# A decay mix with a routed low-rank layer: half of the base product of the first two groups computed early, stored, and added to by DMA

## What is computed

```
a[t] = a[t-1]*decay + exp(f[t])*f[t]      (forward and backward, the same for b with exp(f[t]))
y    = sigmoid(x) * (a_fwd + a_bwd + ...) / (b_fwd + b_bwd + ...) * gain
h      = silu(y @ rw1.T + rb1)                       64 hidden channels
logits = h @ rw2.T + rb2 + gates                     16 experts, top 2, softmax -> coeff
xa     = y @ A.T                                     256 = 16 experts x rank 16
out    = x + y @ W.T + bias + (xa * coeff) @ B.T
```

## Time and profile before

| | |
|---|---|
| median of 3 runs | 720.68 us (720.63 to 720.79) |
| profiled execution, its own time | 720.62 us |
| its span in the trace | 718.8 us |
| busy: PE, DVE, POOL, ACT | 597.5 (83%), 528.0 (73%), 352.2 (49%), 349.3 (49%) us |
| matmuls | 2626 |

### The profile page before, as it was taken

One profiled execution on the slowest core, in us unless ns is written; L12 is line 12 of the kernel. 1 busy time (PEld: TensorE's weight loads), 2 busy tenths in 40 slices (PEclk: granted clock), 3 DMA queues, 4 the chain that ended last, 5 costly groups with the idle time before them and its releaser, 6 DMA issues.

```text
span 718.8 us, 6928 instructions
## 1 busy us (share of the span) xinstructions
PE 597.5 (83%) x2626; PEld 486.8 (68%) x2626; DVE 528.0 (73%) x547; ACT 349.3 (49%) x401; POOL 352.2 (49%) x164
## 2 busy tenths in 40 slices
PE   0005342498999999999999999999999999999998
PEld 0003231386888688868886888778887888888886
DVE  7999999799788979796979796979698713021302
ACT  4777876845574556435664565356735420002000
POOL 1789988744754575356536553655464511000100
PEclk9999665599999999999999999999999999999999
DMA  5324442313350435041613261226214310231031
GB/s 181 117 86 143 141 142 88 118 59 117 127 167 30 146 103 191 29 147 59 224 41 120 86 208 56 74 104 209 83 50 138 95 55 1 88 110 38 0 89 73
DMA packets 30865, 74.22 MB, mean 103 GB/s; under 512 B 4464, under 2 KB 4592, under 8 KB 30832
## 3 DMA queue, kind: packets, MB, share of 16 engines
q1 hardware_dynamic: 30832, 73.79, 30.8%
HBM read 57.00 MB, written 16.78 MB: 103 GB/s over the span
## 4 chain that ended last, share of the span: by engine, by line
PE 59%; DVE 16%; POOL 16%; issue 6%; ACT 2%; DMA 0%; DVEq 0%; SPq 0%; POOLq 0%; ACTq 0%
PE acc L707 18%; PE acc L708 18%; PE acc L709 18%; POOL mix L461 5%; DVE mix L534 4%; DVE yr L560 3%; POOL kv L451 3%; POOL yr L456 3%; POOL y_lo L465 2%; POOL wx_lo L471 2%; DVE mix L539 2%; DVE xo L567 2%; PE acc L719 2%; PE acc L718 2%; ACT y_hi L314 1%
## 5 line engine op out<-in xcount | busy, mean ns | idle before, releaser
L707 PE MATMUL acc<-y_hi,wa_hi 128*128 128x512 f32 x640 | 257.3, 402 | 10.5 <-DVE xo L567 10.5
L708 PE MATMUL acc<-y_lo,wa_hi 128*128 128x512 f32 x640 | 253.5, 396 | 0.0
L709 PE MATMUL acc<-y_hi,wa_lo 128*128 128x512 f32 x640 | 253.2, 396 | 0.0
L707 PEld LDWEIGHTS acc<-y_hi,wa_hi 128*128 128x128 f32 x640 | 123.0, 192 | 43.6 <-DVE xo L567 18.2
L709 PEld LDWEIGHTS acc<-y_hi,wa_lo 128*128 128x128 f32 x640 | 122.7, 192 | 26.4
L708 PEld LDWEIGHTS acc<-y_lo,wa_hi 128*128 128x128 f32 x640 | 123.0, 192 | 24.9
L461 POOL TENSOR_TENSOR mix<-mix,kv 128x1024 f32<-128x1024 f32 x31 | 74.1, 2390 | 90.6 <-DVE mix L518 73.7
L718 PE MATMUL acc<-y_hi,wr 128*128 128x512 f32 x64 | 27.3, 426 | 99.3 <-POOL wa_lo L439 63.6
L567 DVE SCALAR_TENSOR_TENSOR xo<-acc,bias_sb,xo 128x512 f32<-128x512 f32 x64 | 46.7, 736 | 76.5 <-PE acc L709 76.4
L465 POOL TENSOR_TENSOR y_lo<-yr,y_hi 128x1024 fp32r<-128x1024 f32 x32 | 76.6, 2395 | 49.9 <-ACT y_hi L314 49.9
L471 POOL TENSOR_TENSOR wx_lo<-xa,wx_hi 128x512 fp32r<-128x512 f32 x16 | 20.4, 1298 | 152.6 <-ACT wx_hi L373 152.6
(11 more groups left out here) (85 smaller groups left out, 767.4 us busy)
## 6 DMA issues: line engine op xcount, KB each, us to landing
kv<-f_cm SPq DMA_DIRECT2D x32, 512.0 KB, 3.3
yr<-x_cm SPq DMA_DIRECT2D x32, 512.0 KB, 3.3
xo<-x_cm SPq DMA_DIRECT2D x64, 256.0 KB, 4.0
out<-xo SPq DMA_DIRECT2D x64, 256.0 KB, 3.5
xo<-w_base SPq DMA_DIRECT2D x5, 512.0 KB, 3.5
xa<-w_base SPq DMA_DIRECT2D x3, 512.0 KB, 4.3
xa<-w_router_a SPq DMA_DIRECT2D x2, 480.0 KB, 3.4
xo<-w_expert SPq DMA_DIRECT2D x1, 512.0 KB, 3.8
```

The source lines that it names most:

```text
L707: nc.tensor.matmul(out_ap, wh, yh, start=start, stop=False)
L708: nc.tensor.matmul(out_ap, wh, yl, start=False, stop=False)
L709: return nc.tensor.matmul(out_ap, wl, yh, start=False, stop=stop)
```

## The change

- TensorE first computes the base product of groups 0 and 1 (16 output blocks, "parts" p) over kc = 0 to 3 only: parts 0 to 4 as the units arrive, parts 5 to 15 one after the other, each when a bank has been drained (`part_out`).
- ScalarE copies each part from PSUM to `xo[2 + p % 4]` (`drain_part`) in steps 4 to 7; the copies stand after `exp_k` or at the end of the step (`part_steps`). SyncE stores each to `out` (`store_part`).
- Groups 0 and 1 then compute the base product only over kc = 4 to 7 (`base_from`). Their evacuated blocks are no longer stored by SyncE but added to `out` by an accumulating DMA that GpSimd issues (`add_out`), 3 at the end of step q = 2 and 5 at the end of the step in which the group ends, behind `p1(s+1)`.
- Groups 0 and 1 have 3 steps each: G0 in steps 8 to 10, its blocks 3 to 7 in step 11; G1 in 11 to 13, its blocks 3 to 7 in step 14; step 15 has no group; from G2 (step 16) on all is as before. Late splits start with unit 17.
- All even groups run `hid`, both `low_rank` and base block 0 with kc outermost, base block 0 three kc behind; its last three kc come after `spread`. Base block 2 comes before `spread` in even groups.

```diff
-banks = [(0, 1, 2, 3, 4)]
+banks = [(1, 2, 3, 4, 0)]
+
+SPLIT = 2
+HALF = CB // 2
+PARTS = SPLIT * CB
+PBUF = 4
+part_steps = {4: (0, 0, 2), 5: (2, 5, 7), 6: (7, 10, 12), 7: (12, 15, 16)}
+
+def base_from(G):
+    return HALF if G < SPLIT else 0
+
+def first_step(G):
+    return (CB, CB + 3)[G] if G < SPLIT else CB + 4 * G
+
+def last_step(G):
+    return first_step(G) + (3 if G < SPLIT else 4)
+
+tasks_at = {first_step(G) + q: (G, q) for G in range(GROUPS) for q in range(3)}
+ends_at = {last_step(G): G for G in range(GROUPS)}
+
+def quarter(s):
+    return tasks_at.get(s, (-1, -1))
+
+def held(g):
+    return g >= 2 * CB and g % CB in (1, 5)
+
+def stores_to(slot, end):
+    return sum(1 for e in range(PARTS, end) if e % XBUF == slot)
...
-def quarter(g):
-    return divmod(g - CB, 4) if g >= CB else (-1, -1)
...

     def load_x(e):
         if e >= XBUF:
-            sp.wait_ge(out_stored[e % XBUF], 16 * (e // XBUF))
+            if e - XBUF < PARTS:
+                sp.wait_ge(out_added[e % XBUF], 16 * (e // XBUF))
+            else:
+                sp.wait_ge(out_stored[e % XBUF], 16 * stores_to(e % XBUF, e))
         sp.dma_start(xo[:, e % XBUF, :], at(x_cm, e)).then_inc(x_in[e % XBUF], 16)

     def store(e):
         if e + AHEAD < GROUPS * CB:
             load_x(e + AHEAD)
-        sp.wait_ge(evacuated, e + 1)
-        sp.dma_start(at(out, e), xo[:, e % XBUF, :]).then_inc(out_stored[e % XBUF], 16)
+        if e >= PARTS:
+            sp.wait_ge(evacuated, e + 1)
+            sp.dma_start(at(out, e), xo[:, e % XBUF, :]).then_inc(out_stored[e % XBUF], 16)
+
+    def store_part(p):
+        sp.wait_ge(part_out, p + 1)
+        sp.dma_start(at(out, p), xo[:, 2 + p % PBUF, :]).then_inc(part_stored[p % PBUF], 16)
         sp.dma_start(dst, src).then_inc(late_in, 16)
     for s in range(STEPS):
-        if q == 2 and G < GROUPS:
+        ended = ends_at.get(s, -1)
+        early = 5 if ended < SPLIT else 6
+        if ended >= 0:
+            for j in range(3, early):
+                store(ended * CB + j)
+        if q == 2:
             store(G * CB)
         if 1 <= s < UNITS - 1:
             load_k(s + 1)
+        if s - 1 in part_steps:
+            for p in range(part_steps[s - 1][1], part_steps[s - 1][2]):
+                store_part(p)
         for n in chunks_at(load_steps, s):
             load_chunk(n)
-        if q == 0 and G > 0:
-            for j in range(6, CB):
-                store((G - 1) * CB + j)
-        if q == 2 and G < GROUPS:
-            for j in range(1, 3):
-                store(G * CB + j)
+        if ended >= SPLIT:
+            for j in range(early, CB):
+                store(ended * CB + j)
+        if q == 2:
+            store(G * CB + 1)
+            if G >= SPLIT:
+                store(G * CB + 2)
         if 1 <= s < UNITS - 1:
             load_r(s + 1)
+        if s in part_steps:
+            for p in range(part_steps[s][0], part_steps[s][1]):
+                store_part(p)
         for n in chunks_at(load_late_steps, s):
             load_chunk(n)
+        if 0 <= ended < SPLIT:
+            for j in range(early, CB):
+                store(ended * CB + j)
+        if q == 2 and G < SPLIT:
+            store(G * CB + 2)
         if s == CB:
             sp.wait_ge(w_lo_ready, CHUNKS - 1)
+            for i in range(PBUF):
+                sp.wait_ge(part_stored[i], 16 * (PARTS // PBUF))
             for e in range(AHEAD):
                 load_x(e)
     for i in range(XBUF):
-        sp.wait_ge(out_stored[i], 16 * len(range(i, GROUPS * CB, XBUF)))
+        sp.wait_ge(out_added[i], 16 * len(range(i, PARTS, XBUF)))
+        sp.wait_ge(out_stored[i], 16 * stores_to(i, GROUPS * CB))
...
+    def drain_part(p):
+        act.wait_ge(part_done, p + 1)
+        if p >= PBUF:
+            act.wait_ge(part_stored[p % PBUF], 16 * (p // PBUF))
+        nc.scalar.copy(xo[:, 2 + p % PBUF, :], acc[:, p % 5, :]).then_inc(part_out, 1)
+
...
-        late_split = s > 0 and (s - 1) % CB in (1, 5) and s > CB
+        routed = G >= 0
+        late_split = held(s - 1)
...
+        if s in part_steps:
+            for p in range(part_steps[s][0], part_steps[s][1]):
+                drain_part(p)
         if s < UNITS and q != 1:
             sigmoid_r(s)
             exps()
+        if s in part_steps:
+            for p in range(part_steps[s][1], part_steps[s][2]):
+                drain_part(p)
         if 0 < s <= UNITS and late_split:
             split_hi(s - 1)

...
+    def add_out(e):
+        pool.wait_ge(evacuated, e + 1)
+        pool.wait_ge(part_stored[e % PBUF], 16 * (e // PBUF + 1))
+        nc.gpsimd.dma_start(at(out, e), xo[:, e % XBUF, :], accum_op=ALU.add).then_inc(out_added[e % XBUF], 16)
+
...
             p1(s + 1)
+        ended = ends_at.get(s, -1)
+        if 0 <= ended < SPLIT:
+            for j in range(3, CB):
+                add_out(ended * CB + j)
+        if q == 2 and G < SPLIT:
+            for j in range(3):
+                add_out(G * CB + j)
         if s == CB - 2:
...
-        routed = 0 <= G < GROUPS
-        ending = q == 0 and G > 0
+        routed = G >= 0
+        ended = ends_at.get(s, -1)
+        ending = ended >= 0
         if ending:
-            evacuate(G - 1, 3)
-            evacuate(G - 1, 4)
+            evacuate(ended, 3)
+            evacuate(ended, 4)
...
+        if a == 1 and kc < base_from(G):
+            last.then_inc(slot_free, 1)
...
-        return three(acc[:, out_bank(G, j), :], wa_hi[:, kc, c], wa_lo[:, kc, c], yh, yl, kc == 0, False)
+        return three(acc[:, out_bank(G, j), :], wa_hi[:, kc, c], wa_lo[:, kc, c], yh, yl,
+                     kc == base_from(G), False)
+
+    def base_part(p, kc):
+        G, j = divmod(p, CB)
+        yh, yl = y_of(G, kc)
+        c = slice(ER + j * P, ER + (j + 1) * P)
+        last = three(acc[:, p % 5, :], wa_hi[:, kc, c], wa_lo[:, kc, c], yh, yl, kc == 0, kc == HALF - 1)
+        if kc == HALF - 1:
+            last.then_inc(part_done, 1)

...
+    for kc in range(HALF):
+        unit_in(0, kc)
+        pe.wait_ge(w_lo_ready, base_chunk[kc] + 1)
+        for p in range(5):
+            base_part(p, kc)
+    for p in range(5, PARTS):
+        pe.wait_ge(part_out, p - 4)
+        for kc in range(HALF):
+            base_part(p, kc)
+
+    def bank_in(G, n):
+        if G:
+            pe.wait_ge(evacuated, (G - 1) * CB + 4 + n)
+        else:
+            pe.wait_ge(part_out, PARTS - 4 + n)
+
     for G in range(GROUPS):
-        if G == 0:
+        k0 = base_from(G)
+        LAG = 3
+        if G % 2 == 0:
             for kc in range(CB):
                 unit_in(G, kc)
-                pe.wait_ge(w_lo_ready, router_a_chunk[kc] + 1)
+                if G == 0:
+                    pe.wait_ge(w_lo_ready, router_a_chunk[kc] + 1)
+                if kc == 0:
+                    bank_in(G, 0)
                 hid(G, kc)
-                low_rank(G, 0, kc)
-                low_rank(G, 1, kc)
-                pe.wait_ge(w_lo_ready, base_chunk[kc] + 1)
+                for a in range(2):
+                    if kc == 0:
+                        bank_in(G, 1 + a)
+                    low_rank(G, a, kc)
+                if kc - LAG >= k0:
+                    if kc - LAG == k0:
+                        bank_in(G, 3)
+                        if G == 0:
+                            pe.wait_ge(w_lo_ready, base_chunk[CB - 1] + 1)
+                    base(G, 0, kc - LAG)
+            bank_in(G, 4)
+            for kc in range(k0, CB):
+                base(G, 1, kc)
+            if G == 0:
+                pe.wait_ge(late_in, 16 * 7)
+            logits(G)
+            pe.wait_ge(xa_copied, 2 * G + 1)
+            for kc in range(k0, CB):
+                base(G, 2, kc)
+            pe.wait_ge(xa_copied, 2 * G + 2)
+            for a in range(2):
+                spread(G, a)
+            for kc in range(CB - LAG, CB):
                 base(G, 0, kc)
-            pe.wait_ge(late_in, 16 * 7)
         else:
-            first = 5 if G % 2 == 0 else CB
-            pe.wait_ge(evacuated, (G - 1) * CB + 4)
-            for kc in range(first):
-                unit_in(G, kc)
+            bank_in(G, 0)
+            for kc in range(CB):
                 hid(G, kc)
             for a in range(2):
-                pe.wait_ge(evacuated, (G - 1) * CB + 5 + a)
-                for kc in range(first):
+                bank_in(G, 1 + a)
+                for kc in range(CB):
                     low_rank(G, a, kc)
-            for kc in range(first, CB):
-                unit_in(G, kc)
-                hid(G, kc)
+            bank_in(G, 3)
+            for kc in range(k0, CB):
+                base(G, 0, kc)
+            logits(G)
+            bank_in(G, 4)
+            for kc in range(k0, CB):
+                base(G, 1, kc)
+            pe.wait_ge(xa_copied, 2 * G + 2)
             for a in range(2):
-                for kc in range(first, CB):
-                    low_rank(G, a, kc)
```

(50 more changed lines are left out.)

## The result

735.72 us (734.91 to 736.75, 4 runs) against 720.68: ratio 1.021, interval 1.019 to 1.023. The forecast was 725.6 in a range of 718.2 to 731.5: slower, as said, but by 15.0 us and not 5.0. The profiled execution of after took 736.75 (span 735.0), so its span is 16.2 us longer.

A forecast was written before the change was run, and what follows sets the result against it. The prediction took VectorE's scans, then its way from logits to block 7, as the bound. Its terms, -3.4 (shift of G2 without adds), +5.0 (adds) and +3.4 (order), made +5.0 on 720.6: 725.6 us, range 718.2 to 731.5.

The forecast's parts named there:

- parts and drains, to the routing of G1: Early parts, their drains and stores cost 0; the routing of G1 starts at 204.3 us.
- What bounds: VectorE sets steps 8 to 16, so the 43.6 us taken from TensorE don't show.
- c: Time one accumulating DMA holds GpSimd: taken as 1.0 us, between 0.33 and 3.5.
- Plus 5c: Step 15: five adds stand ahead of the sum and gate that ratio(14) needs at once, costing 5.0 us.
- In steps 11, 12 and 14 the adds of the step before hide behind the waits for out3 or the routing, up to c = 1.6.: GpSimd's adds cost nothing in those steps up to 1.6 us each; out3 is the end of block 3's expert product.
- The order of the even groups: 15 more matmuls before the logits make G4's logits 3.4 us later; G6 costs 0.
- The clock: TensorE's half clock after idle: 1.2 us each in G0 and G1, 1.5 at G2.
- Loads of x: Groups 0 and 1: loads waiting for adds cost 0, with an add's own time taken as 5 us.
- Released after all: Rival: TensorE finishes block 3 before VectorE asks, so those waits don't arise: 715.9 us; faster, under 719.2, chance 0.18.
- the accumulations are slow: Rival: evacuations wait for x, or GpSimd's queue carries over: 730 us, beyond 738; with late parts, above 728, chance 0.18.
- late parts: Rival: at half clock parts miss their drains, ScalarE and scans wait, 731 or more; with slow accumulations, chance 0.18.
- two signs of being wrong: Step 16 starting before 270, or block 7 of G3 to that of G4 taking 74.6 us and not 78.

The follow-up runs named there:

- plain stores: The changed kernel with the 16 blocks of groups 0 and 1 stored by SyncE, not added by GpSimd (early half missing from the result): 725.63 us, ratio 1.006.
- hold-back run: The changed kernel with one wait more: in step 12 GpSimd starts sum_n(11) only when the routing's last result is there: 734.22 us, ratio 1.018.
- adds in the gaps: The changed kernel with the same 16 adds moved to GpSimd's idle places, behind gate_n and behind split_lo: 725.78 us, ratio 1.006.
- old order too: The changed kernel with the adds in GpSimd's idle places and TensorE's old order for groups 4 and 6: 720.30 us, ratio 1.000.

## Why the prediction was right in direction and wrong in size

The time lies above the range of 718.2 to 731.5 (by the prediction's own terms the low end is 718.4). By the profiled executions, against the kernel before where a row has no other forecast:

| step of the prediction | forecast | measured |
|---|---|---|
| parts and drains, to the routing of G1 | 0 (204.3) | +1.3 (205.6) |
| routing of G1 to step 13 | 17.05 | 21.3: **+4.3** |
| step 13 to step 15 | 35.7 | 34.9: -0.8 |
| five adds in step 15 | 5c = 5.0 | 7.8 (step 15 is 21.5, not 18.7): **+2.8** |
| y of unit 15 to the routing of G2 | 10.4 | 11.9: +1.5 |
| G2 to G3 | 0 | +1.9 |
| G3 to G4, the order | +3.4 | +3.4 |

The deviations add up to 11.0 of the 11.2 us between the forecast and the span's 16.2 (the G3 to G4 row deviates by 0).

- *What bounds.* Right. Steps 8 to 16 are VectorE's, and the 43.6 us taken from TensorE did not show: it waited for y of units 14 and 15 (16.4 and 8.7 us), as said, and block 3 held VectorE 3.58 and 2.56 us (forecast 3.4 and 2.9).
- *c.* Right for one add alone: 0.9 against 1.0, though it was taken between bounds and not from a row of such a DMA. One step that failed is "Plus 5c": c is not one number. With plain stores step 15 takes 13.76 us (the prediction's 13.7), so the five adds cost 7.8 and not 5.0. The fourth and fifth add waited for room in the descriptor buffer, which the run with 1536 bytes took away. A price per instruction was taken where a resource with a depth stood behind it.
- *"In steps 11, 12 and 14 the adds of the step before hide behind the waits for out3 or the routing, up to c = 1.6."* This failed too, and is the larger miss: +4.3. The delayed `gate_n` did come before `ratio` wanted it (ratio(11) has no wait in step 12), which is all that such a bound asks. But `sum_n` and `gate_n` then ran beside the routing, and two of VectorE's smallest instructions took 4.3 us more together. The hold-back run shows it. The Trainium skill, "SBUF — State Buffer", section "Who interferes with whom", says that VectorE's second pair of ports is GpSimd's only one, that whoever issues first keeps it for its whole instruction, that a cast can take it, and that a `tensor_tensor` with two SBUF inputs contends with a GpSimd instruction that reads SBUF. The trace agrees: each of the two ended within 0.04 us of GpSimd's operation.

  The trace of the kernel before had an instance already. In step 9 an operation of 128x4, 0.17 us in the seven later groups, took 1.59 and ended with GpSimd's operation (145.43 and 145.41):

```profile
143.84 1.59 DVE L593 TENSOR_TENSOR gap<-top 128x4 f32<-128x4 f32 x1
...
143.05 2.36 POOL L445 TENSOR_TENSOR wb_lo<-xa,wb_hi 128x1024 fp32r<-128x1024 f32 x1
```

- *The order of the even groups.* Right to 0.1 us, in after, in the kernel before with the order alone, and by its absence when undone. G6 costs nothing, as said: 3.4 us more to G6, 3.4 less to G7.
- *The clock.* The prediction allowed 1.2 us after each of the idle stretches in G0 and G1 and 1.5 at G2, and nothing behind them: a term put at nothing without a reason. The way to the routing of G2 took 1.5 more, and G2 to G3 1.9. TensorE's timeline of after, blocks 5 and 6 of G2:

```profile
325.04 0.50 PE L790 MATMUL acc<-y_hi,wa_hi 128*128 128x512 f32 x1 [3.75 <-DVE xo L649]
...
328.47 0.63 PE L791 MATMUL acc<-y_lo,wa_hi 128*128 128x512 f32 x1
328.90 0.63 PE L792 MATMUL acc<-y_hi,wa_lo 128*128 128x512 f32 x1
```

The matmuls come 0.43 apart there, at the lower of the two clocks (1.2 and 2.4 GHz; the stretch 324 to 334 had a mean granted clock of 0.66). The new order makes that idle stretch, 3.75 us, since it leaves TensorE 15 matmuls fewer between logits and evacuation: G4 has none with the old order, and the kernel before has it in G2 and G4 once it is given the new one. How long the clock stays low behind it differs with the same idle time. In this execution the 9 us behind the stretch in G2 have a mean granted clock of 0.62, in G4 0.81, and the way to the next routing is 76.4 and 74.5 us; in the kernel before with the new order it is the other way round (0.81 and 0.62; 74.6 and 76.5).

  Several kernels with the early parts also spread widely: 721.5 to 727.1 over 9 runs (adds in the gaps), 717.2 to 722.9 over 10 (old order too), the kernel before 720.6 to 721.3 over 17. The idle stretch alone does not explain it, since the kernel before with the new order has it and stays within 0.14 us in its 4 runs. The cause of the spread stays open.
- *Loads of x.* Right: the adds landed in 5.6 us, and no evacuation waited for a load.
- *The rivals.* "Released after all" was out by 3.58 and 2.56 us of waiting; late parts were out too. The measured time falls to "the accumulations are slow" and late parts, above 728, with a chance of 0.18. Half of that rival's condition came true: one add landed in 5.6 us and not 7.5, but five of them held GpSimd for 7.5 us, 1.5 each and so above its 1.3, and "GpSimd's own queue carries over into more steps" is what happened in step 12. It named the event and not its cost, the small VectorE instructions that were held. Neither of the prediction's two signs of being wrong came up: step 16 started at 283.4, and G3 to G4 was 78.

Open: 1.2 us up to step 10, which the prediction put at 0 ("The stores of parts stand behind loads that have over 5 us to spare"). In steps 5 to 8 ScalarE waits 0.5 to 0.9 us each for f, which it did not in the kernel before, and in step 8 VectorE waits 2.84 us for ScalarE's `low_rows` (2.21 before). Drains and later loads of f both lie ahead of it, and no run parted them. With plain stores, the larger buffer or the old order for groups 4 and 6 the routing of G1 still came at 204.3 to 204.4, the forecast: there TensorE's clock behind the idle stretch of G0 took less than the 1.2 us allowed (mean granted clock 0.81 to 0.84 over 9 us in two of them, 0.65 in after), block 3 held VectorE 2.5 us and not 3.58, and the two errors cancel.

## What to carry to other kernels

Work moved off the engine that is busy by share gains only what the stage's own bound lets through: first ask what places the waits of that stage. Here the split paid (0.991) only after the evacuations that held VectorE and the logits of G1 were moved as well. When instructions are added to an engine, follow not only who waits for it, but what its delayed operations then run beside, and how many of them its buffers take at once. And look in the trace of the kernel before for small instructions that take far longer in one place than in all others: they show where one engine holds up another.

## What the runs showed of the hardware

- One accumulating DMA of 256 KB (128 x 2 KB) holds GpSimd 0.9 us (after). With 1024 bytes of descriptor buffer three go at once, and the fourth and fifth pause 1.7 us each (1.4 and 2.2 at the end of step 11); with 1536 five go at once (4.47 us). From issue to landing 5.6 us, a plain store from SyncE 4.2 in the same run.
- VectorE instructions of 0.17 us took 2.54 and 2.08 beside a GpSimd `tensor_tensor` of 128x1024 (after), 2.23 with the larger buffer, and 1.59 in the kernel before; beside the issue of a DMA the cast kept its 0.17 (`sum_n` held back).
- Behind the same idle stretch of 3.75 us TensorE's mean granted clock over 9 us was 0.62 in one group and 0.81 in another of one execution.
